# Attention with a mixture of experts: each group of heads takes the second half of its queries first

## The reference, cut to what matters

```python
scores = jnp.einsum('bqhd,bkhd->bhqk', q, k) * attn_scale[0]
scores = jnp.where(mask[None, None], -jnp.inf, scores)     # mask in chunks of 64: a query sees later keys
attn = jax.nn.softmax(scores, axis=-1)
out = jnp.einsum('bhqk,bkhd->bqhd', attn, v).reshape(B, T, C)
x = layernorm(x + out @ Wo.T + bo)
x = layernorm(x + moe(x))     # 32 experts of width 64, top 6 by group, and a shared one
```

## Time and profile before

| | |
|---|---|
| median of 3 runs | 441.92 us (441.58 to 442.02) |
| profiled execution | 443.63 us, its span 441.6 us |
| busy share of the span | PE 93%, DVE 78%, ACT 51%, POOL 31% |
| granted TensorE clock, mean | 0.948 of 2.4 GHz |

### The profile page before, as it was taken

One profiled execution on the slowest core, in us unless ns is written; L12 is line 12 of the kernel. 1 busy time (PEld: TensorE's weight loads), 2 busy tenths in 40 slices (PEclk: granted clock), 3 DMA queues, 4 the chain that ended last, 5 costly groups with the idle time before them and its releaser, 6 DMA issues.

```text
span 441.6 us, 8102 instructions
## 1 busy us (share of the span) xinstructions
PE 411.4 (93%) x2870; PEld 216.7 (49%) x2870; DVE 343.4 (78%) x775; ACT 226.8 (51%) x309; POOL 134.9 (31%) x257
## 2 busy tenths in 40 slices
PE   5659999999999999999989989999999999999993
PEld 2424434343333334334334446766776776666661
DVE  4969988898989898989954564976778768778863
ACT  4610077775778696877777784232432253332220
POOL 5000236685575666566554250000000000000000
PEclk9955579999999999999999998999999999999997
DMA  4565141120303012020000007333222233334430
GB/s 122 187 206 162 41 125 53 33 81 7 106 4 88 27 40 74 25 76 6 3 3 4 1 29 122 107 115 96 91 92 105 92 105 95 126 95 128 135 95 24
DMA packets 27391, 34.51 MB, mean 78 GB/s; under 512 B 5912, under 2 KB 16472, under 8 KB 27352
## 3 DMA queue, kind: packets, MB, share of 16 engines
q1 hardware_dynamic: 27016, 33.34, 25.6%
q10 hardware_dynamic: 336, 0.66, 0.5%
HBM read 29.33 MB, written 4.65 MB: 77 GB/s over the span
## 4 chain that ended last, share of the span: by engine, by line
PE 79%; DVE 13%; ACT 3%; issue 2%; DMA 1%; ACTq 1%; SPq 0%; POOL 0%; DVEq 0%; POOLq 0%
PE ps L1248 16%; PE ps L1350 13%; PE ps L1205 11%; DVE mx L907 10%; PE ps L1318 7%; PE ps L1320 7%; PE ps L1319 7%; PE ps L1229 7%; PE ps L1209 3%; ACT probs L805 2%; PE ps L1271 2%; PE ps L1283 1%; ACTq L542 1%; DMA bk<-in_bk 1%; PE ps L1171 1%
## 5 line engine op out<-in xcount | busy, mean ns | idle before, releaser
L907 DVE TENSOR_REDUCE mx<-ps 128x1 f32<-128x512 f32 (+3 forms) x304 | 179.5, 656 | 23.2 <-PE ps L1209 19.2
L805 ACT ACTIVATE probs<-ps 128x1024 f32<-128x1024 f32 (+2 forms) x160 | 143.4, 940 | 51.6 <-PE ps L1229 51.1
L1205 PE MATMUL ps<-rows_k,rows_q 48*128 48x512 bf16 (+3 forms) x384 | 103.0, 361 | 11.2 <-DMA rows_k<-scratch 7.1
L847 ACT ACTIVATE rows_q<-ps 128x512 f32<-128x512 f32 x68 | 40.6, 599 | 93.3 <-PE ps L1320 92.5
L1248 PE MATMUL ps<-probs,Vg 128*32 128x512 f32 (+3 forms) x768 | 82.5, 502 | 0.3 <-POOL probs L705 0.3
L1229 PE MATMUL ps<-rows_q,rows_k 51*128 51x512 bf16 (+3 forms) x384 | 71.5, 334 | 2.7 <-ACT probs L805 2.1
L1318 PE MATMUL ps<-x1hi,w_hi 128*128 128x512 f32 x136 | 73.9, 543 | 0.1
L1129 DVE TENSOR_TENSOR rows_k<-ps,rows_q 128x512 f32<-128x512 f32 x64 | 43.9, 686 | 34.5 <-PE ps L1350 34.1
L1205 PEld LDWEIGHTS ps<-rows_k,rows_q 48*128 48x128 bf16 x384 | 30.1, 96 | 80.8 <-DVE mx L907 65.0
L1350 PE MATMUL ps<-rows_q,w_down 128*128 128x512 f32 x136 | 69.7, 594 | 0.0
L701 POOL TENSOR_SCALAR_AFFINE_SELECT probs<-probs 64x512 f32<-64x512 f32 x64 | 42.3, 661 | 77.9 <-ACT probs L805 76.8
(11 more groups left out here) (107 smaller groups left out, 332.9 us busy)
## 6 DMA issues: line engine op xcount, KB each, us to landing
comb_rows<-weights SPq DMA_DIRECT2D x128, 128.0 KB, 3.0
scratch<-oT SPq DMA_DIRECT2D x8, 384.0 KB, 3.3
w_raw<-in_unitT SPq DMA_DIRECT2D x17, 128.0 KB, 2.4
rows_q<-scratch SPq DMA_DIRECT2D x16, 96.0 KB
rows_k<-scratch SPq DMA_DIRECT2D x14, 96.0 KB
w_down<-in_unitT SPq DMA_DIRECT2D x1, 1088.0 KB, 5.9
xT<-in_xT SPq DMA_DIRECT2D x4, 256.0 KB, 4.4
rows_q<-scratch SPq DMA_DIRECT2D x16, 64.0 KB
```

Source lines behind the costliest of these rows:

```text
L805: act.activation(dst, src, ACT.Exp).then_inc(exps_ready, 1)
L907: dve.tensor_reduce(dst, src, AX.X, ALU.max).then_inc(max_read, 1)
L1205: mm = pe.matmul(bank(max_bank(k), m, at), q, rows_k[r0:r0 + ROWS_QK, s, j * T + k0:j * T + k0 + m], start=True, stop=not first, tile_posi ...
```

## The change

Every group now takes part 1 (second 512 queries) ahead of part 0, in the maxima, in the tops and their stores, in the exponentials and in the values. The unit with four pieces (tile 7 and the last keys of tile 3) moves to part 1, so that part 1 has 12 maxima units and part 0 has 26 (before: part 0 came first and had 28, part 1 had 10). The join is made after the first unit of the next group. A top goes out 5 units after its part instead of 4. The first four blocks, with 1280 query columns of 4608, are all on the diagonal. The 16 projections of v leave the gaps between those of q and k: three follow the last projection, three wait for DVE's sixth split part, three for the seventh, and seven for the eighth.

```diff
+PART_ORDER = (1, 0)
+def nth_top(g, part):
+    return 2 * g + PART_ORDER.index(part)
...
-    if part == 0:
+    if part == 1:
         units.append([(j, q, P * last if q == last else P * q + BANK, P, b * 2 * P + j * P, q == last)
...
-        for part in range(2):
+        for part in PART_ORDER:
...
-TOP_AFTER = 4
+TOP_AFTER = 5
...
-    return [(kt, 0) for kt in lower] + [(kt, 1) for kt in range(KT - 1, KT // 2 - 1, -1)]
+    return [(kt, 1) for kt in range(KT - 1, KT // 2 - 1, -1)] + [(kt, 0) for kt in lower]
...
-LOWER = KT
+LOWER = KT // 2
...
+VALUES_AT_PARTS = {3: 6, 6: 7, 9: 8}
...
             for g in range(NG):
-                store_max(g, 0)
+                store_max(g, 1)
                 if g == 0:
                     load_rows(2)
-                store_max(g, 1)
+                store_max(g, 0)
...
-                if part == 1 and k == LAST_OF[g, 0] + 1:
-                    dve.wait_ge(max_read, READS_THROUGH[k - 1])
+                if k - 1 == LAST_OF.get((g - 1, 0)) or k == LAST_OF[NG - 1, 0]:
+                    dve.wait_ge(max_read, READS_THROUGH[k if k == LAST_OF[NG - 1, 0] else k - 1])
...
-                if n == 1:
-                    pe.wait_ge(wv_loaded, 16)
-                if n >= 1:
-                    project_values(2 * n - 2)
-                    project_values(2 * n - 1)
-            project_values(NT - 2)
-            project_values(NT - 1)
+            pe.wait_ge(wv_loaded, 16)
+            for t in range(NT):
+                if t in VALUES_AT_PARTS:
+                    pe.wait_ge(parts_ready, VALUES_AT_PARTS[t])
+                project_values(t)
```

More of the change, by code:

```diff
@@ L146 @@
 POOL_RANK = {"first": 0, "split": 1, "values": 2, "bias": 2, "unit": 3, "mask": 4}
-BETWEEN_MASKS = [c for c in range(LOWER) if DIAGONAL[c]][:3]
+BETWEEN_MASKS = [c for c in range(LOWER, NB) if DIAGONAL[c]][:3]
 def attention_order():
@@ L275, in attention_order @@
                 m_done[n] = dve
-                if n - 1 == LAST_OF[g, 0]:
+                if n - 1 == LAST_OF.get((g - 1, 0)) or n == LAST_OF[NG - 1, 0]:
                     dve += 150
-                    joined[g] = dve + hop
+                    joined[g if n == LAST_OF[NG - 1, 0] else g - 1] = dve + hop
             else:
@@ L612, in store_max @@
                 s = g % NS
-                sp.wait_ge(max_split, 2 * g + part + 1)
+                sp.wait_ge(max_split, nth_top(g, part) + 1)
                 r0 = g % GPB * STRIP + 2 * part
@@ L616, in store_max @@
                 sp.dma_start(region.rearrange("h c (q p) -> (c q) h p", p=P), mh[:, part, :, :]).then_inc(max_stored, 16)
-                sp.wait_ge(max_stored, 16 * (2 * g + part + 1))
+                sp.wait_ge(max_stored, 16 * (nth_top(g, part) + 1))
                 for half_ in range(2):
@@ L725, in split_top @@
                 if g >= 1:
-                    pool.wait_ge(max_stored, 16 * (2 * g + part - 1))
-                n, top = 3 * (2 * g + part), mn[:, part, :]
-                pool.wait_ge(tops_copied, 2 * g + part + 1)
+                    pool.wait_ge(max_stored, 16 * (nth_top(g, part) - 1))
+                n, top = 3 * nth_top(g, part), mn[:, part, :]
+                pool.wait_ge(tops_copied, nth_top(g, part) + 1)
                 pool.tensor_copy(mh[:, part, 0, :], top).then_inc(max_split_steps, 1)
@@ L809, in copy_top, with copy_output @@
                 if g >= 1:
-                    act.wait_ge(max_split, 2 * g + part - 1)
-                act.wait_ge(tops_ready, 2 * g + part + 1)
+                    act.wait_ge(max_split, nth_top(g, part) - 1)
+                act.wait_ge(tops_ready, nth_top(g, part) + 1)
                 act.activation(mn[:, part, :], bank(max_bank(k), P)[0:PART_KEYS, :], ACT.Copy,
                                scale=-1.0).then_inc(tops_copied, 1)
-            def copy_output(g, h):
-                act.wait_ge(values_used, NB * g + (NB if h else LOWER))
+            def copy_output(g, second):
+                h = 0 if second else 1
+                act.wait_ge(values_used, NB * g + (NB if second else LOWER))
                 act.copy(oT[:, g, h * BANK:(h + 1) * BANK], bank(VALUES)).then_inc(output_copied[h], 1)
@@ L897, in reduce @@
                 if g >= 1 and k in PART_STARTS:
-                    dve.wait_ge(tops_ready, TOPS_THROUGH[k] if part else 2 * g - 1)
+                    dve.wait_ge(tops_ready, 2 * g - 1 if part else TOPS_THROUGH[k])
                 dve.wait_ge(max_scores, READS_THROUGH[k])
@@ L1240, in values @@
                     if g >= 1:
-                        pe.wait_ge(output_copied[1], g)
+                        pe.wait_ge(output_copied[0], g)
                 elif c == LOWER:
-                    pe.wait_ge(output_copied[0], g + 1)
+                    pe.wait_ge(output_copied[1], g + 1)
                 pe.wait_ge(exps_ready, NE * g + EXPS_UP_TO[c])
@@ L1263, in tail_step @@
                 else:
-                    pe.wait_ge(output_copied[1], NG)
+                    pe.wait_ge(output_copied[0], NG)
                 if kind == "out":
```

## The result

The changed kernel takes 452.90 us, the median of 4 runs (451.68 to 454.53); the kernel before took 441.75 beside it (4 runs, 441.06 to 442.02). The ratio is 1.0262, with a 95% interval from 1.0243 to 1.0281: 11.6 us slower, where 2.9 us faster was forecast. It is the slowest of its four runs, with a mean granted clock of 0.935 against 0.943 to 0.946 in the others. A run more than 1.5% above the fastest of its kernel counts as slow, and every ratio here is of the fast runs alone.

A forecast was written before the change was run, and what follows sets the result against it. The start was taken as bound by DVE, then by a slow PE, and steady groups by the two coupled. Terms 0.2 + 2.2 + 0.5 = 2.9 us off 441.92 gave 439.0 us, range 436.5 to 446.

The forecast's parts named there:

- The end: After the last maxima: fewer exponentials and value columns left for PE and ACT, 0.5 us saved, 0 to 1.6.
- The clock: PE's granted clock from 24 to 62 us: forecast to stay at 1.00, chance 0.36, giving 439.0 us.
- Rival B: Start: clock stays at 1.2 GHz through the second half's products too; 444.5 us (442.5 to 446.5), chance 0.22.
- rival A: Start: clock falls in the maxima and comes back with the first values; 440.8 us (439 to 442.5), chance 0.23.
- the 2.2 + 0.2: Forecast gains at the start: 2.2 us of DVE's waits in group 0, 0.2 us from moving v tiles in the opening.
- rival C: Start of group 0: part 1's rows come late at SP, up to 1.6 us lost; 440.6 us, chance 0.05.
- Rows of the maxima: Group 0: exponentials may wait 0 to 3.4 us for loaded rows, DVE loses 0 to 1.6 us; taken as 0.
- Opening: Before the first maxima: taking the v tiles from between the projections gains 0 to 0.2 us; taken as 0.2.
- Steady groups: Later attention groups, same work in another order: taken as 0, with 1.5 us faster to 2.4 slower.
- the prediction's sign: Whole kernel: 2.9 us faster forecast, with chances 0.50 faster, 0.24 same, 0.26 slower.

The follow-up runs named there:

- experiment 1: Changed kernel with the comb step alone moved back ahead of value product 9 on PE and the last copy of values on ACT: 442.46 us, ratio 1.0048.
- experiment 2: Kernel before with the comb step alone at its late place, behind value product 10 and, on ACT, the last copy of values: 449.93 us, ratio 1.0166.
- experiment 3: Changed kernel with DVE making the low part of x1 of quarter 1 ahead of its product with the router weights: 450.01 us, ratio 1.0198.
- experiment 4: Changed kernel with 18 unused products on PE ahead of the first down product: 452.99 us, ratio 1.0216.
- experiment 9: Unused PE products added: ahead of first maxima, changed kernel, 451.58 us; behind early maxima units, four new- and old-order kernels, 493.24, 457.51 to 498.29, 469.73, 478.97 us.
- experiment 5: Changed kernel with SP's five transfers of constants behind part 1's store and group 2's loads, not ahead of them: 450.14 us, ratio 1.0204.
- experiment 8: Old order, placed v tiles, x1 low part earlier on DVE: 440.83 us (0.9988); changed kernel, comb and SP's constants moved, same DVE move: 443.05 us (1.0036).

## Why the prediction was wrong

*The end: the step that failed.* The last group was priced by PE's and ACT's work (0.5 us saved, 0 to 1.6), and "the experts' stage, from 264 us on, is untouched, so I look at attention only" took the rest out of view. But the planner's order holds the router's steps too, and the change moved comb behind two value products and the up products that go with them. The move adds no work on PE, which is why a sum over PE's work could not see it; the cost is in the trip behind it: store, load, DVE, PE in order behind DVE (4.97 us of wait instead of 1.04), and the low clock behind that wait (6.8 us instead of 3.4). Measured size of the step: 2.14% in the new order (experiment 1), 1.66% in the old (experiment 2), some 9.4 and 7.3 us. None of my rivals had it, and the range ended at 446.0. The order was read at the start of group 0, and not at its last steps.

*The clock.* Forecast at 1.00 from 24 to 62 us (0.36); it fell near 28.7 and rose at 73.1. Rival B was the right mechanism in this execution (low still at the seventh exponential unit, which came at 66.4 us instead of 60.0), and in its way: the second half's products, 512 to 128 columns wide, ran from 50.5 to 59.1 us without a rise, and the clock rose 2.6 us after the first product of part 0 began (70.50 us), where it had been 3.1 before. In experiments 3 and 4 it rose with the second half's products, as in rival A, fell again, and was low at the seventh exponential unit all the same. B's price, 2.6 + 2.9 us for the start less the 2.2 + 0.2 that no longer came, is 3.1 us against before; measured were 4.5 at unit 77 (2.7 to 4.7 over the four profiles with these instructions), with rival C in it. The Trainium skill ("TensorE: Matmul & The Clock Gate", "HAM oscillation") warns of idle gaps and advises to order loops so that PE stays warm. For this kernel that was not enough by the trace and experiment 9: with the gap filled the clock fell at 29.1 us, and a PE busy 15.00 of 15.00 us stood at 0.50.

*Rows of the maxima.* Taken at 0, with 1.6 as upper bound. The first exponentials came at 45.87 instead of 44.7. I had taken 2.0 us from a row of a later store to the issue of its load; here the store took 2.85 and the loads were issued by 44.6, not 43.1. As a delay that was inside the bound, but the price was not: repaired, it gave 2.6 us in experiment 5, and 1.5 on top of experiment 1, there with intervals that overlap. C had 0.05 and was priced as if it could not come together with B.

*Opening.* 0 to 0.2 us forecast; the placed v tiles gave 0.3% (0.1 to 0.5), some 1.2 us, in the old order. Right in sign, but the like kernel of experiment 8 shows 0.1% with 0 in its interval, so the size is open.

*Steady groups.* Forecast 0, with 1.5 faster to 2.4 slower. Four of them came to 24.98 us where those before took 25.06 to 25.44: a gain of 0.1 to 0.4 us each, given back in the one group of 26.93. Right. One reading under it was not: 0.82 x 25.0 = 20.5 us is PE's share of the chain, not its work, which is 24.30 of 25.00 us by its busy time in that group; no number of the forecast rests on it.

*Together.* With both side effects repaired the new order is 0.1 to 0.4% above before (1.0014 and 1.0036), and 0.5% above the old order with placed v tiles: about 2 us slower, where I had forecast 2.9 faster. With the comb alone put right it is 0.5% above before (experiment 1), so the prediction's sign would have been wrong even then. That B and C account for this rest is argued from the profiles, not shown by a run; the size of the miss is the comb, and that is shown.

## What to carry to other kernels

When a planner writes the order, read what it did to every stream, above all to steps that it places "when ready": a step of no cost on its own engine can head a chain through memory, and its place is priced by what waits at the other end. An instruction that needs nothing should not stand in an in-order queue behind one that waits for a transfer (experiment 3). And two rivals that make the same engine late are not alternatives: price them together. Of what was run, the old order with the v products placed is the best, 440.69 us against 441.76; the like kernel of experiment 8, at 0.9988, shows how small that is.

## What the hardware showed unexpectedly

The clock did not follow from the program alone. The changed kernel and experiments 1, 3 and 4 have the same instructions up to the last group, and their low clock at the start ended at 73.1, 72.8, 54.1 and 55.1 us. The kernel before and experiment 2 share theirs too, and it ended at 61.2 and 66.0 us. This moves times by some us: unit 77 was done 2.0 us apart among the first four (79.0 to 81.0). A stretch of one profile, or of a pair, can therefore not show what an edit did to the clock.

In the changed kernel PE was busy 14.5 of 15 us from 29 to 44 us at 0.50, and with the products of experiment 9 15.00 of 15.00, so a busy PE neither held nor raised it. In none of the 15 profiles with a low clock there did it rise between 30 us and the first value product. In 13 of them it rose 1.8 to 8.0 us after the first value product over 512 queries had begun; in the other two, the changed kernel and experiment 1, the second half's four products passed without a rise, and it came 2.6 and 1.9 us after the first product of part 0. What decides between these is open.

In the kernel before, over all sets, 12 runs with a mean clock of 0.954 took 440.0 to 441.8 us, 26 with 0.948 took 440.7 to 443.3: part of the ordinary spread goes with the clock.

A transfer of the router weights out and back (store issued to first use on DVE) took 5.3 us in experiment 1, 5.7 in the changed kernel, 6.5 in the kernel before, 6.9 in experiment 3 and 7.2 in experiment 4, though the transfers are the same.
